# Experts of a two-branch attention kernel: value sums copied by the scalar engine, two sums of the out-projection on GpSimd, another order per engine, late quarters one round later

## The reference, cut to what matters

```
xn = layernorm(x);  out = x + encoder(xn) + experts(xn)

experts(x):                                   # 8 heads of 16 columns, 4 experts of 64 rows each
  for e in 0..3:                              # expert e sees rows 64e..64e+63 and the first m = 128 >> e columns
    xm = layernorm(x[rows e])[..., :m]
    q, k, v [rows e] = xm @ (q_w, k_w, v_w)[:, :m].T + bias
  attn = softmax(q k^T / sqrt(128));  a = attn @ v          # over all 256 rows, not causal
  for e in 0..3:
    o[rows e] = pad(a[rows e, :m] @ o_w[:m, :m] + o_b[:m])  # columns from m on are zero
  return o + x
```

## Time and profile before

| what | value |
|---|---|
| median of three runs | 1580.44 us |
| profiled execution, its own time | 1580.7 us |
| its span, first to last instruction | 1578.6 us |
| TensorE busy over the span | 1423.4 us, 90% |
| ScalarE / VectorE / GpSimd busy | 1219.6 (77%) / 1087.0 (69%) / 609.2 us (39%) |
| mean granted TensorE clock | 0.973 |
| expert scores, first and last slot's last block of `pv` | 64.1 us, 304.2 us |
| first maxima of the encoder | 315.65 us |

### The profile page before, as it was taken

The page is one execution under the profiler, slowest core; times in us unless marked ns, Lnnn a source line. Parts: engine busy times, 40 slices in busy tenths (PEclk is TensorE's granted clock), DMA queues, the critical chain, the costliest instruction groups (busy, mean ns, idle before and its releaser), DMA issues.

```text
span 1578.6 us, 39453 instructions
## 1 busy us (share of the span) xinstructions
PE 1423.4 (90%) x10594; PEld 939.3 (60%) x10720; DVE 1087.0 (69%) x2850; ACT 1219.6 (77%) x2165; POOL 609.2 (39%) x1055
## 2 busy tenths in 40 slices
PE   2678888689999999999999999999999999999995
PEld 1445555346666666666666666666666666666653
DVE  5576777456767777777777767777777777777762
ACT  3233343248989999999999989999999999899883
POOL 4332333323333333333333333333333345555433
PEclk9998999879999999999999999999999999999997
DMA  6333333144444444544444445444445455454430
GB/s 167 92 88 94 106 104 109 43 122 121 123 123 130 125 124 127 146 132 122 122 123 133 129 123 141 133 126 121 120 130 135 128 135 136 130 135 132 125 92 11
DMA packets 106535, 187.78 MB, mean 119 GB/s; under 512 B 20105, under 2 KB 72457, under 8 KB 106449
## 3 DMA queue, kind: packets, MB, share of 16 engines
q1 hardware_dynamic: 91632, 150.45, 34.9%
q0 software_dynamic: 14848, 36.72, 8.7%
HBM read 120.87 MB, written 65.01 MB: 118 GB/s over the span
## 4 chain that ended last, share of the span: by engine, by line
PE 68%; DVE 12%; issue 8%; DMA 4%; ACT 3%; POOL 2%; SPq 1%; DVEq 0%; POOLq 0%; ACTq 0%
PE pvp L1128 15%; PE exp_ps L1105 10%; PE mxp L1071 10%; DVE negm L801 9%; PE dense L1169 6%; PE mxp L1017 6%; PE mxp L1075 5%; PE dense L1046 4%; PE dense L1157 3%; DMA blocks<-split_L 3%; PE mxp L1079 2%; PE mxp L1056 2%; PE dense L1017 2%; PE mxp L1146 2%; PE mxp L1046 2%
## 5 line engine op out<-in xcount | busy, mean ns | idle before, releaser
L801 DVE TENSOR_REDUCE negm<-mxp 128x2 f32<-128x512 f32 x896 | 570.1, 686 | 76.8 <-PE mxp L1075 57.5
L965 ACT ACTIVATE probs<-exp_ps 128x512 f32<-128x512 f32 x896 | 511.8, 592 | 132.1 <-PE exp_ps L1105 129.2
L1105 PE MATMUL exp_ps<-qbd_l,kst_l 128*128 128x512 f32 x768 | 346.8, 479 | 14.1 <-ACT exp_ps L990 9.6
L1071 PE MATMUL mxp<-blocks,qst 104*128 104x512 f32 x768 | 333.8, 468 | 7.7 <-DMA blocks<-split_L 6.9
L990 ACT ACTIVATE exp_ps<-masktf 128x512 f32<-128x512 f32 x513 | 308.7, 602 | 23.1 <-DVE rest L873 6.9
L611 POOL TENSOR_TENSOR lo<-y,hi 128x512 fp32r<-128x512 f32 x80 | 102.6, 1283 | 328.6 <-DVE hi L776 328.6
L1128 PE MATMUL pvp<-probs,vst_l 128*32 128x256 f32 (+1 forms) x4096 | 207.6, 332 | 10.3 <-issue 10.0
L1075 PE MATMUL mxp<-maskb,identb 128*128 128x256 bf16 (+1 forms) x642 | 197.7, 308 | 0.0
L1071 PEld LDWEIGHTS mxp<-blocks,qst 104*128 104x128 f32 x768 | 148.4, 193 | 50.9 <-issue 33.6
L1128 PEld LDWEIGHTS pvp<-probs,vst_l 128*32 128x32 f32 x4096 | 111.1, 109 | 95.3 <-issue 36.9
L1075 PEld LDWEIGHTS mxp<-maskb,identb 128*128 128x128 bf16 x768 | 75.1, 98 | 150.4 <-issue 135.3
(11 more groups left out here) (102 smaller groups left out, 1902.6 us busy)
## 6 DMA issues: line engine op xcount, KB each, us to landing
split_L<-hi SPq DMA_DIRECT2D x256, 128.0 KB, 2.1
qst<-split_L SPq DMA_DIRECT2D x64, 384.0 KB
kst_l<-split_L SPq DMA_DIRECT2D x64, 384.0 KB
qbd_l<-split_L SPq DMA_DIRECT2D x256, 96.0 KB
split_L<-lo POOLq DMA_DIRECT2D x128, 128.0 KB, 2.3
blocks<-split_L POOLq DMA_DIRECT2D x128, 96.0 KB, 4.3
blocks<-split_L SPq DMA_DIRECT2D x128, 96.0 KB
split_F<-hi SPq DMA_DIRECT2D x64, 128.0 KB, 2.1
```

What stands on the lines that cost most here:

```text
L801: dve.tensor_reduce(heads[:, g, first:first + count], bank[MAX_BANK + k % 3].rearrange("p (h t) -> p h t", h=count), AX.X, ALU.max, negate ...
L965: act.activation(probs[:, g, ch, :], exp_ps[:, k % 2, :], ACT.Exp, scale=plan.scale).then_inc(q.b_exp, 1)
L1071: pe.matmul(o, qst[0:BIAS_END, g, qt * P:(qt + 1) * P], kbd[0:BIAS_END, first:first + count, g, 0:keys], start=True, stop=True, skip_group ...
L1105: last = pe.matmul(o, kst[plan.name][:, s, g, kt * P:(kt + 1) * P], rhs, start=seeder not in ("ACT", "DVE"), stop=True, skip_group_check=True)
```

## The change

In the experts' list of steps another order and other units; other banks; `pv+` goes from VectorE to ScalarE; the second and third sum of `op+` go from VectorE to GpSimd; `v` and `v+` are no longer among the encoder's early steps; the statistics of quarters 2 and 3 run after round 0 instead of after slot -1, their norms after round 1 instead of after round 0, and GpSimd's clearing of the query buffers is placed with them.

```diff
@@ slot_steps, the experts' part
-                at("rstd ln", s + 2) + at("v+", s + 1) + at("op", s - 2) + at("stack>", s + 1) + at("hi>", s + 2)
-                + at("pv+", s - 1) + at("row> v", s + 1) + at("xn", s + 2) + at("ot+", s - 1) + at("xt+", s + 2)
-                + at("at+ ot", s - 1) + at("xt", s + 2)
-                + part("exp", s, 0, 1) + at("at", s - 1) + at("qk", s + 2) + part("pv", s, 0) + at("y", s + 2)
-                + at("xb", s - 2)
-                + part("exp", s, 2, 3) + at("op+", s - 2) + at("lo hi", s + 2) + part("max", s + 1, 0)
-                + at("stackp", s + 2) + part("max", s + 1, 1)
-                + part("exp", s, 4) + part("max", s + 1, 2, 3)
-                + part("exp", s, 5, 6) + part("max", s + 1, 4, 5) + part("pv", s, 1) + part("max", s + 1, 6)
-                + part("exp", s, 7) + part("max", s + 1, 7) + part("pv", s, 2, 3) + at("negt+ negt", s + 1))
+                part("pv", s - 1, 2) + at("ln", s + 2) + at("stack> v", s + 1) + part("pv", s - 1, 3)
+                + at("pv+", s - 1) + at("rstd xt", s + 2) + at("ot", s - 1) + at("row>", s) + at("xn", s + 2)
+                + at("op", s - 2) + at("xb", s - 1) + at("v+", s + 1) + at("negt+", s) + at("xt+", s + 2)
+                + at("ot+", s - 1) + at("y qk", s + 2) + at("op+", s - 2) + at("hi", s + 2) + part("max", s + 1, 0)
+                + part("exp", s, 0) + part("max", s + 1, 1) + at("lo", s + 2)
+                + part("exp", s, 1) + part("max", s + 1, 2)
+                + part("exp", s, 2) + part("max", s + 1, 3)
+                + part("exp", s, 3) + part("max", s + 1, 4, 5) + at("stackp", s + 2)
+                + part("exp", s, 4) + part("max", s + 1, 6)
+                + part("exp", s, 5) + part("max", s + 1, 7)
+                + part("exp", s, 6) + at("at", s - 1)
+                + part("exp", s, 7) + part("pv", s, 0, 1) + at("hi>", s + 2) + at("at+", s - 1) + at("negt", s + 1))
@@ banks, early steps
-    "xt": 2, "qk": 2, "v": 1, "at": 0, "op": 4, "negt": 3, "ot": 0})
+    "xt": 2, "qk": 4, "v": 3, "at": 1, "op": 0, "negt": 4, "ot": 3})
-EARLY = ("ln", "rstd", "xn", "xt", "xt+", "qk", "y", "hi", "lo", "hi>", "v", "v+")
+EARLY = ("ln", "rstd", "xn", "xt", "xt+", "qk", "y", "hi", "lo", "hi>")
@@ GpSimd
+                    elif step == "op+" and not plan.causal:
+                        pool.wait_ge(q.c_add, u + 1)
+                        settle(pool, passed_pool)
+                        pool.tensor_tensor(tmp[:, s, :, :], tmp[:, s, :, :], seg_cols[:], ALU.mult).then_inc(q.c_add2, 1)
+                        pool.wait_ge(q.c_add2, u + 1)
+                        pool.wait_ge(q.c_xb, u + 1)
+                        settle(pool, passed_pool)
+                        pool.tensor_tensor(rest[:, u, :, :], tmp[:, s, :, :], xb[:, s, :, :], ALU.add).then_inc(q.c_done, 1)
...
+            def clear_more_queries():
+                clear_queries(1)
+                clear_queries(2)
...
-                          (None, second_half_of_deviations, lambda: clear_queries(1), lambda: clear_queries(2)))
+                          (None, None, second_half_of_deviations, clear_more_queries))
@@ VectorE
-                    elif step == "pv+":
+                    elif step == "pv+" and plan.causal:
...
+                            wait_past(dve, q.c_done, u - 1)
                             bias = wc["F"][:, C_BO:C_BO + D].unsqueeze(1).to_broadcast([P, NT, D])
                             dve.tensor_tensor(tmp[:, s, :, :], projected, bias, ALU.add).then_inc(q.c_add, 1)
-                            dve.wait_ge(q.c_add, u + 1)
-                            dve.tensor_tensor(tmp[:, s, :, :], tmp[:, s, :, :], seg_cols[:], ALU.mult).then_inc(q.c_add2, 1)
-                            dve.wait_ge(q.c_add2, u + 1)
-                            dve.wait_ge(q.c_xb, u + 1)
-                            dve.tensor_tensor(rest[:, bt, :, :], tmp[:, s, :, :], xb[:, s, :, :], ALU.add).then_inc(q.c_done, 1)
...
-                dve.wait_ge(s_w, 16 * 3)
...
-                          (lambda: first_norm(1), second_half_of_statistics, second_half_of_norms, None))
+                          (lambda: first_norm(1), lambda: dve.wait_ge(s_w, 16 * 3), second_half_of_statistics, second_half_of_norms))
@@ ScalarE
+                    elif step == "pv+" and not plan.causal:
+                        act.wait_ge(q.b_pv, GROUPS * (u + 1))
+                        wait_past(act, q.c_ot, u - 1)
+                        act.activation(ost[:, s, :, :].rearrange("p r t -> p (r t)"), pvp[:, :], ACT.Copy).then_inc(q.c_ost, 1)
```

## The result

The changed kernel takes 1555.19 us (median of four runs, 1552.4 to 1556.56); the kernel before, beside it, 1580.36. The ratio is 0.9845, 95% interval 0.982 to 0.9869: faster by 1.6%, where 1.1% was forecast (1563), and inside the range. The profiled execution took 1555.07, with a span of 1553.0.

The account below looks back on a forecast made before the run. A chain of waits between engines was taken to bound the expert slots. Gains 8.5 (opening), 14.9 (slots 0 to 13), 1.6, 3.1 (slots 14, 15), less 9.1 (end), made 19.0: 1561.7, stated as 1563 us, range 1551 to 1576.

Parts of the forecast that it names:

- the relay: Expert slot: TensorE idles 1.55 and 0.70 us between VectorE's steps; new order fills this, slot 13.05 before added costs.
- The copy: Expert slot: copy of `ost` on ScalarE, in its queue ahead of `xt+`, taken at 0.60 us.
- Two sums on GpSimd: Expert slot: third loop closes at 13.0 to 13.5 us; second sum overlaps `hi`, costing it 0.4.
- Clock: Expert slots: lower granted clock costs 0 to 1.0 us a slot; half and half with GpSimd's overlap gives 0.7.
- 4.0 after slot 3: Slots 0 to 13: norms of eight batches (4.4 us) after slot 3 add 4.0 us.
- Opening: Up to slot 0: without two quarters' statistics `xn`(2) starts earlier, double block of pv at 55.6; gain 8.5 us.
- Slot 15: Slot with the encoder's first steps in front: row of maxima loses 2.2, exponentials save 3.6; gain 3.1 us.
- The end: Into the encoder: GpSimd's clearing of `blocks` waits behind unit 15's `op+` and the whole tail; loss 9.1 us.
- C: Rival: clock or a late row of maxima eats half; slots 14.4 to 15.3, 1571 to 1576 us; chance 0.18.
- D: Rival: slower, GpSimd's queue becomes the bound; slot 15.7, reaching 1587 us, break-even slot 15.3; chance 0.06.
- A: The forecast itself: slots 13.3 to 14.4, sum 11 to 26, 1555 to 1570 us; chance 0.55.
- B: Rival: GpSimd's sums dodge `hi`, clock stays high; slots 13.05, 1551 to 1555 us; chance 0.14.

Follow-up runs that it names:

- the order alone: Changed order, banks and early steps on the kernel before, with its engines and quarters kept: 1553.04 us, ratio 0.9852.

## Why the prediction was right

- *The mechanism, the relay replaced by pv 2 and 3:* right, and shown: the order alone gives slots of 14.10, with the copy on ScalarE and the sums on VectorE 12.78 (the working said 13.05 before the costs of the overlap and the clock). The loops of TensorE and VectorE do close together: `xt` waited 0.2 to 0.4 us for `xn` in six of nine slots.
- *The copy, 0.60:* measured 0.60.
- *Two sums on GpSimd:* the overlap with `hi` was forecast at 0.4; where it occurs `hi` takes 1.00, not 0.83. It occurs in seven of the nine slots from 4 to 12. The Trainium skill's lock ("SBUF — State Buffer", section "SBUF: two separate sides"), by which whichever of the two starts first has the ports for its whole instruction, is what the runs come close to. At 208.07 GpSimd's sum starts first, keeps its 0.73, and `hi` ends 0.3 behind it (208.80, 209.09); at 221.50, where the two start within 0.005 us, `hi` keeps its 0.43 and the sum is stretched to 1.02. Either way the pair takes 1.02 us, against 1.16 if one ran wholly after the other, and the norms lose nearly the clearings' time. I had found the rule and still took the milder number from `xn`.
- *Clock:* the mis-sized term of the slot. I added 0.5 for the low clock in every second slot; it was 1.00 throughout. Its price was too high as well: before the change the slots with a slow `qk` took 15.65 to 15.72 us and the others 15.07 to 15.11, 0.6 apart and not 1.0. That also bounds what the clock gave of the 2.2 us a slot: some 0.3 on average. The slot adds up otherwise: 12.78 with the sums on VectorE, plus 0.57 in seven of nine slots, is 13.22; measured 13.23.
- *The clearings beside the norms:* missed. I counted 4.0 after slot 3; it was 8.2 (21.48 less a slot), 3.5 of them the overlap with GpSimd again. The part worst forecast for its size.
- *Opening:* 3.5 better than said. 2.3 of these are not the change's: the second quarter of the input was used from 10.97 us before and from 8.69 after, and over the fourteen profiles from 8.69 to 11.73. From `hi` of slot -1 on the opening is 27.8 and 18.1, a gain of 9.7 against 8.5.
- *Slot 15:* 1.6 too hopeful. `exp` 0 waited 1.93 us for the row of maxima, until 265.34, and the scores behind it ran at the low clock (granted 0.50 from 262 to 271.5 us; a block of 128x512 took up to 0.79 us, in the slots up to 0.51).
- *The end:* right in kind and nearly in size, 10.0 against 9.1, and confirmed by two separate runs.
- *The prices of the rivals:* C's slots of 14.4 to 15.3 give 1570 to 1581 by the forecast's own sum, not 1571 to 1576; 15.3 is the break-even that D names. The opening adds up to 55.4, not 55.6. Neither changes the forecast.

The errors had both signs, and part of the closeness is luck. The time lies at the edge between A and B, but the slots (13.23) are just below A's 13.3 and above B's 13.05: it is a mixture of faster slots, a slow slot 3, a lucky opening, and an encoder (1260.1 us) beside one of before near the top of its scatter (1263.0). Without the last two, 5.2 us, the two spans differ by 20.4, against the 19.0 of the sum.

## What to carry to other kernels

When a chain of short steps on several engines bounds a pipelined loop, split a block of work that is already ready and put its halves where the chain makes TensorE wait; then move off an engine only what stands in front of the chain there (the copy, 1.2 us a slot), not what fills its waits (moving the sums made a slot 0.5 us longer). Before work goes to another engine's queue, look at what stands behind it at the stage's end: one late item there cost 8 to 10 us, as much as four or five slots had gained. And keep GpSimd's instructions away from VectorE's normalisations and casts: here the overlap cost a cast 0.57 us and sixteen norms 3.5.

## What the runs showed of the hardware that was not expected

- A GpSimd clearing cost VectorE's norms nearly its whole length, once: 16 norms took 4.18, 5.94 and 7.71 us with none, one (1.8) and two (3.57) clearings beside them.
- Moving the copy and the sums off VectorE in the old order made the slots longer (16.27 us instead of 15.46), with the granted clock of the stage at 0.88 instead of 0.94. With the copy alone they were 15.67 and 0.94; the cause of the rest is open.
- VectorE could start on the second quarter of the input between 8.7 and 11.7 us after the start in fourteen profiles; differences under 3 us in such an opening need a second anchor.
